# A decoder layer on one Trainium2 core: the causal mask of the scores written by ScalarE instead of by mask matmuls

## The chip, the core and the metric

The kernel runs on one core of a Trainium2 chip. A core has five engines that run their own instruction streams and meet at semaphores: TensorE (PE in the profile; its weight loads are listed as PEld), VectorE (DVE), ScalarE (ACT), GpSimd (POOL) and SyncE (SP), which here only starts transfers. The metric is the device time of one execution in microseconds, the median of several runs.

## The reference

A batch of 64 sequences of 128 tokens, 128 wide, goes through one decoder layer: a causal convolution, a minimal GRU and a feed-forward block (the mixer), a cross-attention, and a mixture of experts, each with a residual and a layer norm. The change is in the cross-attention: 16 heads of width 64, 128 queries against 120 context rows, with a causal mask that adds -1e10 above the diagonal before the softmax. Cut to that part:

```python
q = (query @ Wq + bq).reshape(B, T, H, Dk)          # query = x, T = 128
k = (key @ Wk + bk).reshape(B, S, H, Dk)            # key = value = context, S = 120
v = (value @ Wv + bv).reshape(B, S, H, Dv)
q = q * (1.0 / jnp.sqrt(jnp.asarray(Dk, q.dtype)))
scores = jnp.einsum('bthd,bshd->bhts', q, k)
causal = jnp.tril(jnp.ones((T, S), scores.dtype))
scores = scores + NEG_INF * (1.0 - causal)
attn = jax.nn.softmax(scores, axis=-1)
ctx = jnp.einsum('bhts,bshd->bthd', attn, v).reshape(B, T, H * Dv)
out = ctx @ Wo + bo
```

## The kernel before, in words

The 64 sequences are worked in 16 groups of four. Three stages run as a software pipeline: in one body the group `b` is in attention, the next group `a = b + 1` is in the mixer, and the group before, `c = b - 1`, is in the mixture of experts. The `pipeline` helper (L198) calls `body(a, b, c)` for each engine; 14 of the 16 bodies with a group in attention have all three stages. There is no scheduler: the order of the work on each engine is the order of the calls in that engine's `body`, written out by hand, and each engine issues strictly in that order.

The attention of a group has a projection part (24 projections, L353, evicted from PSUM by ScalarE for even numbers and by VectorE for odd ones, L650 and L916) and then ten steps `s` = 0 to 9. The eight steps 0 to 7 each make one score pair `p = s`: a sequence (p // 2) and one half of its heads. The two PSUM banks `sE` and `sO` (called `score_banks`) hold four heads each, 4 x 120 columns. What a step does, by engine, as far as the change bears on it:

- TensorE, `body` L499: the transposes of the normalized probabilities of pair s - 2 (`b_probs_T`, L396), in even steps the transposes of the experts' output (`c_act_T`, L483), then `b_scores(b, s)` (L373), in step 5 the hidden-state product of the GRU (`a_hid`, L291), then the probabilities times the values of pair s - 2 (`b_pv`, L409), in even steps the experts' down projection (`c_down`, L490), then the experts' up projections (`c_up`, L464), then mixer work (in step 1 `a_pw`, L277, in step 3 a transpose `a_norm_T`), and in odd steps the output projection (`b_wo`, L426). `b_scores` waits until ScalarE has finished the probabilities of the pair before in both banks, writes the mask into each bank with one bfloat16 matmul of an identity with the mask, 480 columns wide (L385), and adds the scores with eight fp32 matmuls (L390).
- VectorE, `body` L1084: copies the transposed probabilities to SBUF (`b_probs_T`, L947), takes the negated row maximum of both score banks (`b_max`, L941), adds a bias to the attention heads (`b_heads_T`, L961), takes reciprocals (`b_recips`, L957), does the experts' gating (`c_experts`, L1054), and mixer pieces: the convolution (`a_conv`, L848) in step 1, the low part of a normalized transpose (`a_norm_low`, L831) in step 3, the GRU's drive (`a_gru_drive`, L868) in step 5. The order within a step is such that the copies for pair s - 2 stand first in step s, behind all that VectorE has to do in step s - 1.
- ScalarE, `body` L730: the exponentials of a pair, bank by bank (`b_probs`, L675: four exponentials with a running sum per bank), the experts' tanh (`c_tanh`, L715: in odd steps between the two banks, in even steps behind the second), the eviction of the experts' transposes in even steps (`c_actT`, L723), and mixer pieces at the end of a step: `a_norm` (L600) ahead of step 0 and in step 3, `a_conv` (L617) in step 0, the squares `a_sums` in step 2, `a_gate` in step 4, `a_hid` (L630) in step 5.
- GpSimd: scales the probabilities by the reciprocals (`b_normal`, L1245) and weights the experts' activations (`c_weight`, L1256). At the start of the program it builds the identity and the mask (L1172 to L1182).

The waits around the change read as follows in the kernel before:

```python
if p:
    pe.wait_ge(sem["probs"], upto("probs", b, 2 * p - 1))
for r in range(2):
    mm(score_banks[r][:, 0:4 * S], identb[:], maskb[:].unsqueeze(1).to_broadcast([P, 4, S]),
       start=True, stop=False, skip_group_check=True)
```

Of the kernel before, what the change touches and what calls it, by code (L numbers as in the profile page):

```python
# [18 lines left out]
ACT = mybir.ActivationFunctionType  # L19
# [6 lines left out]
P = 128  # L26
# [4 lines left out]
S = 120  # L31
# [9 lines left out]
PAIRS = 2 * SEQ  # L41
# [16 lines left out]
    "gru_sum": 1, "gelu": 4, "mixer": 2,  # L58
    "ln1_stats": 4, "ln1_mv": 4, "ln1_eps": 1, "ln1_rstd": 1, "ln1_out": 4, "x1T_hi": 1, "x1T": 1, "x1_bo": 1,

    "ctx_hi": 1, "ctx_split": 1, "proj": 24, "proj_act": 12, "proj_dve": 12, "scores": 16, "negmax": 16, "probs": 16,
    "probsT": 16, "probsT_sb": 16, "rinv": 16, "normal": 16, "pv": 8, "headsT_sb": 8,
    "wo": 4, "attn_sum": 4, "ln2_stats": 4, "ln2_mv": 4, "ln2_eps": 4, "ln2_rstd": 4, "ln2_out": 4,

# [16 lines left out]
def layer_kernel(nc, x, ctxT, w_pw, w_gru, w_ff1, w_ff2, cols, rows, w_q, w_k, w_v, w_o, w_g, w_u, w_rs, w_d, w_sd, out):  # L81
    with ExitStack() as ctx:  # L82
# [3 lines left out]
        sem = {n: ctx.enter_context(nc.semaphore(n)) for n in [*PER_GROUP, *ONCE]}  # L86

        def later(g):

            return not (isinstance(g, int) and g == 0)  # L90

        def upto(name, g, k=0):

            return g * PER_GROUP[name] + (k + 1) * (16 if name.endswith(("loaded", "stored")) else 1)

        def whole(name, g):

            return g * PER_GROUP[name] + PER_GROUP[name]
# [73 lines left out]
        score_banks = [sE, sO]  # L172

        def seqs(ap, n=SEQ):
            return ap.rearrange("p (b n) -> p b n", b=n)
# [67 lines left out]
        def _(pe):  # L243
            mm = nc.tensor.matmul
            pe.wait_ge(sem["mixer_weights"], MIXER_WEIGHTS)
            pe.wait_ge(sem["ident"], 1)
            pe.wait_ge(sem["identb"], 1)
            pe.wait_ge(sem["mask"], 1)

            def turn(dst, src):  # L250
                return nc.tensor.transpose(dst, src, ident[0:src.shape[0], 0:src.shape[0]])  # L251
# [121 lines left out]
            def b_scores(b, p):  # L373
                q, half = p // 2, p % 2
                if p == 0:
                    pe.wait_ge(sem["proj_act"], upto("proj_act", b, 14 // 2))
                    pe.wait_ge(sem["proj_dve"], upto("proj_dve", b, 15 // 2))
                elif p == 1:
                    pe.wait_ge(sem["proj_act"], upto("proj_act", b, 18 // 2))
                    pe.wait_ge(sem["proj_dve"], upto("proj_dve", b, 19 // 2))  # L380
                if p:

                    pe.wait_ge(sem["probs"], upto("probs", b, 2 * p - 1))
                for r in range(2):
                    mm(score_banks[r][:, 0:4 * S], identb[:], maskb[:].unsqueeze(1).to_broadcast([P, 4, S]),  # L385
                       start=True, stop=False, skip_group_check=True)
                for i in range(4):
                    j = 4 * half + i
                    for r in range(2):
                        ins = mm(score_banks[r][:, i * S:(i + 1) * S], qT[r * DK:(r + 1) * DK, j, q * T:(q + 1) * T],  # L390
                                 kT[r * DK:(r + 1) * DK, j, q * S:(q + 1) * S], start=False, stop=True,
                                 skip_group_check=True)
                        if i == 3:
                            ins.then_inc(sem["scores"], 1)
# [172 lines left out]
        def _(act):  # L567
            f = nc.scalar.activation
            act.wait_ge(sem["gammas"], 1)
            act.wait_ge(sem["bq8"], 1)  # L570

            def w_high(names):
                for n in names:
                    if n in LATE_LOADS:
                        act.wait_ge(sem[f"{n}_in"], 16)
                    f(split[n][0][:], raw[n], ACT.Copy).then_inc(sem["w_hi"], 1)
# [73 lines left out]
            def b_project(b, lo, hi):  # L650
                for n in range(lo, hi):
                    if n % 2:
                        continue
                    act.wait_ge(sem["proj"], upto("proj", b, n))
                    src = proj_banks[n]
                    kind, j = projections[n]
                    if n == 12 and not later(b):
                        act.wait_ge(sem["w_lo"], len(SPLIT))
                    if n == 0:

                        if later(b):
                            act.wait_ge(sem["scores"], whole("scores", b - 1))
                    if n == 8:

                        if later(b):
                            act.wait_ge(sem["pv"], whole("pv", b - 1))
                    if kind == "v":
                        ins = f(vv[:, j // 2, (j % 2) * 512:(j % 2) * 512 + 512], src[0:S, :], ACT.Copy)
                    elif kind == "k":
                        ins = f(kT[:, j, :], src[:, 0:SW], ACT.Identity, bias=c_(f"bk{j}"))  # L670
                    else:
                        ins = f(qT[:, j, :], src[:], ACT.Identity, bias=c_(f"bq{j}"), scale=DK ** -0.5)
                    ins.then_inc(sem["proj_act"], 1)

            def b_probs(b, p, r):  # L675
                if p >= RING:

                    act.wait_ge(sem["probsT"], upto("probsT", b, 2 * (p - RING) + 1))
                else:
                    if later(b):  # L680
                        former = max(m for m in range(PAIRS) if m % RING == p)
                        act.wait_ge(sem["probsT"], upto("probsT", b - 1, 2 * former + 1))
                act.wait_ge(sem["negmax"], upto("negmax", b, 2 * p + r))
                for i in range(4):
                    ins = f(pr[:, p % RING, r, i, :], score_banks[r][:, i * S:(i + 1) * S], ACT.Exp,  # L685
                            bias=nm[:, p % 2, r, i:i + 1], accum_out=rsum[:, p % 2, r, i, :])
                ins.then_inc(sem["probs"], 1)
# [42 lines left out]
            def body(a, b, c):  # L730
                A, B, C = a is not None, b is not None, c is not None

                if B:
                    b_project(b, 4, 6)
                if C:
                    c_x2T(c)
                if A:
                    a_sums(a, 0)
                if B:
                    b_project(b, 6, 8)  # L740
                if B:
                    b_project(b, 8, 9)
                    a_x1T(b)
                if C:
                    c_shared(c)
                if B:
                    b_project(b, 9, 13)
                if C:
                    c_router(c)
                if B:  # L750
                    b_project(b, 13, 18)
                    b_probs(b, 0, 0)
                    b_project(b, 18, 20)
                if C:
                    c_sharedT(c)
                if B:
                    b_probs(b, 0, 1)
                if A:
                    a_norm(a, 0)
                for s in range(PAIRS + LAG):  # L760
                    even = s > 1 and s % 2 == 0
                    if C and even:
                        c_actT(c, s // 2 - 1)
                    if B and 0 < s < PAIRS:
                        b_probs(b, s, 0)
                    if C and s < PAIRS and s % 2:
                        c_tanh(c, s)
                    if B and s == 1:
                        b_project(b, 22, 23)
                    if B and 0 < s < PAIRS:  # L770
                        b_probs(b, s, 1)
                    if B and s == 0:
                        b_project(b, 20, 21)
                    if C and s < PAIRS and s % 2 == 0:
                        c_tanh(c, s)
                    if A:
                        if s == 0:
                            a_conv(a)
                        elif s == 2:
                            a_sums(a, 1)  # L780
                            if not later(a):
                                w_high(SPLIT[2:5])
                        elif s == 3:
                            a_norm(a, 1)
                        elif s == 4:
                            a_gate(a)
                        elif s == 5:
                            a_hid(a)
                        elif s == 7:
                            a_sums(a, 2)  # L790
                            if not later(a):
                                w_high(SPLIT[5:])
                        elif s == 8:
                            b_project(a, 0, 2)
                            a_norm(a, 2)
                            b_project(a, 2, 4)
                        elif s == 9:
                            for k in range(FCH):
                                a_gelu(a, k)

            pipeline(act, body)


# [544 lines left out]
```

## Time and profile before

| what | value |
|---|---|
| runs | 1743.06, 1748.45, 1751.35 us; median 1748.45 |
| span of the profiled execution | 1742.6 us (the lowest run is 1743.06) |
| PE busy | 1535.3 us, 88% of the span |
| DVE busy | 1172.2 us, 67% |
| ACT busy | 865.7 us, 50% |
| POOL busy | 724.7 us, 42% |
| mean granted TensorE clock | 0.967 of full speed |

The span runs from the first to the last instruction of one execution. A busy share is an average over the whole span. In a timeline, a line gives the start, the duration, the engine, the source line, the operation with its output and inputs, the count, and in brackets how long the engine had been idle before it and what released it. Line numbers are those of the kernel before.

### The profile page before, as it was taken

Reading aid. Unit: us, or ns where it says so; the run is one execution under the profiler, and the core shown is the slowest. Engines: PE = TensorE matmul, PEld = TensorE weight load, DVE = VectorE, ACT = ScalarE, POOL = GpSimd, SP = SyncE. Lnnn points to the kernel's source line nnn. Section 1 sums busy time; section 2 is a strip of 40 time slices with the busy share of each in tenths; the row PEclk is TensorE's granted clock in tenths of the full one; section 3 lists DMA queues with packets and bytes.
Section 4 is the critical chain, followed back from the end, with each engine's and each line's share of the span. In section 5 each row is a group of like instructions: output and inputs, shape, how many; then the busy total and the mean of one; then the engine's idle time right before and its main releaser. Section 6 shows DMA issues by size and latency. Waiting matters only on the chain. (4 is left out here: it accounts for less than half of the span.)

```text
span 1742.6 us, 35886 instructions
## 1 busy us (share of the span) xinstructions
PE 1535.3 (88%) x11552; PEld 1256.2 (72%) x11552; DVE 1172.2 (67%) x2822; ACT 865.7 (50%) x3177; POOL 724.7 (42%) x882
## 2 busy tenths in 40 slices
PE   2879998999899998998999899999989999899966
PEld 2667777777777776777777777777777777777754
DVE  2566867577685767757677685767767577686642
ACT  3645555364554545455464554545455464554421
POOL 5433534434353534525444353534534444352412
PEclk9999999999999999999999999999999999999987
DMA  3000000000000000000000000000000000000000
GB/s 132 7 7 1 6 14 5 16 2 16 1 5 14 3 15 2 3 14 3 15 2 16 1 5 14 3 15 2 3 14 3 15 2 16 1 5 3 4 4 7
DMA packets 22167, 18.08 MB, mean 10 GB/s; under 512 B 1904, under 2 KB 20912, under 8 KB 22064
## 3 DMA queue, kind: packets, MB, share of 16 engines
q1 hardware_dynamic: 22064, 17.05, 3.1%
q14 instruction: 80, 0.66, 0.1%
q8 instruction: 23, 0.38, 0.1%
HBM read 12.85 MB, written 4.19 MB: 10 GB/s over the span
## 5 line engine op out<-in xcount | busy, mean ns | idle before, releaser
L1247 POOL TENSOR_TENSOR pr<-pr,ri 128x480 f32<-128x480 f32 x256 | 254.5, 997 | 521.5 <-DVE ri L959 521.5
L685 ACT ACTIVATE pr<-sE,nm 128x120 f32<-128x120 f32 x512 | 178.0, 360 | 308.0 <-DVE nm L944 308.0
L422 PE MATMUL pvb<-pT,vv 120*64 120x128 f32 x2048 | 142.2, 282 | 75.4 <-DVE pT L955 75.3
L422 PEld LDWEIGHTS pvb<-pT,vv 120*64 120x64 f32 x2048 | 111.0, 138 | 106.3 <-issue 52.0
L685 ACT ACTIVATE pr<-sO,nm 128x120 f32<-128x120 f32 x512 | 178.7, 378 | 0.0
L1266 POOL TENSOR_TENSOR ew<-e,gw 128x512 f32<-128x512 f32 x128 | 135.7, 1060 | 87.5 <-DVE e L1066 73.6
L955 DVE COPY pT<-t 120x512 f32<-120x512 f32 x256 | 164.1, 682 | 1.3 <-PE t L251 0.9
L390 PEld LDWEIGHTS sE<-kT,qT 64*128 64x128 f32 x1024 | 123.4, 187 | 50.9 <-issue 50.9
L390 PE MATMUL sE<-kT,qT 64*128 64x120 f32 x1024 | 147.0, 284 | 0.0
L390 PE MATMUL sO<-kT,qT 64*128 64x120 f32 x1024 | 147.0, 284 | 0.0
L496 PE MATMUL m<-wd,eT_s 128*128 128x128 f32 x1024 | 136.4, 288 | 2.9 <-ACT eT_s L728 2.9
L496 PEld LDWEIGHTS m<-wd,eT_s 128*128 128x128 f32 x1024 | 124.0, 198 | 14.5 <-issue 10.3
L251 PE MATMUL t<-ident_f,pr 128*120 128x128 f32 x1024 | 133.7, 274 | 0.0
L431 PEld LDWEIGHTS pvb<-wo,hT 128*128 128x128 f32 x1024 | 124.9, 196 | 12.0 <-DVE hT L969 9.0
L431 PE MATMUL pvb<-wo,hT 128*128 128x128 f32 x1024 | 130.0, 281 | 3.1 <-DVE hT L969 3.1
L1058 DVE SCALAR_TENSOR_TENSOR et<-et,m 128x512 f32<-128x512 f32 x128 | 87.6, 685 | 57.5 <-ACT et L721 57.5
L728 ACT ACTIVATE eT_s<-m 128x512 f32<-128x512 f32 x128 | 69.7, 595 | 108.5 <-PE m L251 108.5
L390 PEld LDWEIGHTS sO<-kT,qT 64*128 64x128 f32 x1024 | 123.4, 187 | 0.0
L1252 POOL TENSOR_TENSOR ve<-mv,eps 128x1 f32<-128x1 f32 x128 | 24.4, 190 | 236.5 <-DVE mv L981 181.7
L251 PEld LDWEIGHTS t<-ident_f,pr 128*120 128x120 f32 x1024 | 117.7, 138 | 6.7 <-issue 0.2
L944 DVE TENSOR_REDUCE nm<-sE 128x4 f32<-128x480 f32 x128 | 83.4, 651 | 54.3 <-PE sO L390 54.3
L685 ACT ACTIVATION_READ_ACCUMULATOR pr<-sO,nm 128x1 f32 x512 | 115.5, 226 | 0.0
(271 smaller groups left out, 3914.5 us busy)
## 6 DMA issues: line engine op xcount, KB each, us to landing
xt<-in_x SPq DMA_DIRECT2D x16, 256.0 KB, 2.8
out_y<-y SPq DMA_DIRECT2D x64, 64.0 KB, 1.6
cT<-in_ctxT SPq DMA_DIRECT2D x16, 240.0 KB, 2.9
hT<-in_w_k SPq DMA_DIRECT2D x1, 512.0 KB, 6.6
qT<-in_w_v SPq DMA_DIRECT2D x1, 512.0 KB, 7.4
qT<-in_w_q SPq DMA_DIRECT2D x1, 512.0 KB, 8.2
wo<-in_w_o SPq DMA_DIRECT2D x1, 512.0 KB, 9.1
qT<-in_w_g SPq DMA_DIRECT2D x1, 512.0 KB, 8.8
```

The lines of the kernel that those rows point to most:

```text
L251: return nc.tensor.transpose(dst, src, ident[0:src.shape[0], 0:src.shape[0]])
L390: ins = mm(score_banks[r][:, i * S:(i + 1) * S], qT[r * DK:(r + 1) * DK, j, q * T:(q + 1) * T], kT[r * DK:(r + 1) * DK, j, q * S:(q + 1) * ...
L422: ins = mm(pvb[r * DK:(r + 1) * DK, (k // 2) * T:(k // 2 + 1) * T], vv[:, q, h * DK:(h + 1) * DK], pT[:, 4 * r + k // 2, :], start=True, s ...
L431: ins = mm(pvb[:, 0:P], hT[:, j, :], wo[:, j, :], start=(j == 0), stop=(j == NCH - 1))
L496: mm(m1[:, 0:P], eT[:, j, :], wd[:, j, :], start=(j == 0), stop=False)
L685: ins = f(pr[:, p % RING, r, i, :], score_banks[r][:, i * S:(i + 1) * S], ACT.Exp, bias=nm[:, p % 2, r, i:i + 1], accum_out=rsum[:, p % 2, ...
L728: f(eT[:, 4 * k:4 * k + 4, :], seqs(src[:]), ACT.Copy).then_inc(sem["eT_sb"], 1)
L944: V.tensor_reduce(nm[:, p % 2, r, :], seqs(score_banks[r][:, 0:4 * S]), AX_X, ALU.max, negate=True).then_inc(sem["negmax"], 1)
L955: V.tensor_copy(pT[:, 4 * k:4 * k + 4, :], seqs((t0, t1)[k][0:S, :])).then_inc(sem["probsT_sb"], 1)
L1058: V.scalar_tensor_tensor(et[:], et[:], 1.0, m0[:], ALU.add, ALU.mult).then_inc(sem["e_gate"], 1)
L1247: GP.tensor_tensor(pr[:, p % RING, r, :, :], pr[:, p % RING, r, :, :], ri[:, p % 2, r, :, :].to_broadcast([P, 4, S]), ALU.mult).then_inc(s ...
L1266: GP.tensor_tensor(seqs(ew[:, half * 512:(half + 1) * 512], 8), seqs(e3[:, n % 2, :], 8), gw[:, n // 2, 8 * half:8 * half + 8].unsqueeze(2 ...
```

## The change

ScalarE gets a new function, `b_mask(b, p, r)`: it copies the mask, repeated four times, from SBUF into the 480 columns of score bank `r`, and counts a new semaphore, `masked`. For the pairs after the first it waits for ScalarE's own exponentials of the pair before to be complete in that bank; for the first pair it waits for the eviction of the projection that had the bank (number 12 for `sE`, 13 for `sO`). `b_scores` loses the two mask matmuls and the wait on `probs`, waits for both masks instead, and its score matmuls, unchanged, have `start=False` and so add onto what the bank holds. In ScalarE's order the masks of the first pair stand between the projections 14 and 16, those of pair 1 behind the second bank's exponentials of pair 0, ahead of `a_norm`, and those of pair s + 1 behind the second bank's exponentials of pair s, for s = 1 to 6. The waits on the identity and the mask at the program's start move from TensorE to ScalarE (the mask alone).

```diff
@@ PER_GROUP @@
-    "ctx_hi": 1, "ctx_split": 1, "proj": 24, "proj_act": 12, "proj_dve": 12, "scores": 16, "negmax": 16, "probs": 16,
+    "ctx_hi": 1, "ctx_split": 1, "proj": 24, "proj_act": 12, "proj_dve": 12, "masked": 16, "scores": 16, "negmax": 16, "probs": 16,
@@ tensor @@
-            pe.wait_ge(sem["identb"], 1)
-            pe.wait_ge(sem["mask"], 1)
@@ b_scores @@
-                if p:
-
-                    pe.wait_ge(sem["probs"], upto("probs", b, 2 * p - 1))
-                for r in range(2):
-                    mm(score_banks[r][:, 0:4 * S], identb[:], maskb[:].unsqueeze(1).to_broadcast([P, 4, S]),
-                       start=True, stop=False, skip_group_check=True)
+
+                pe.wait_ge(sem["masked"], upto("masked", b, 2 * p + 1))
@@ scalar @@
+            act.wait_ge(sem["mask"], 1)
...
+            def b_mask(b, p, r):
+                if p:
+                    act.wait_ge(sem["probs"], upto("probs", b, 2 * (p - 1) + r))
+                elif r:
+                    act.wait_ge(sem["proj_dve"], upto("proj_dve", b, 13 // 2))
+                else:
+                    act.wait_ge(sem["proj_act"], upto("proj_act", b, 12 // 2))
+                f(seqs(score_banks[r][:, 0:4 * S]), maskb[:].unsqueeze(1).to_broadcast([P, 4, S]),
+                  ACT.Copy).then_inc(sem["masked"], 1)
@@ scalar body @@
-                    b_project(b, 13, 18)
+                    b_project(b, 13, 15)
+                    b_mask(b, 0, 0)
+                    b_mask(b, 0, 1)
+                    b_project(b, 15, 18)
                     b_probs(b, 0, 0)
                     b_project(b, 18, 20)
                 if C:
                     c_sharedT(c)
                 if B:
                     b_probs(b, 0, 1)
+                    b_mask(b, 1, 0)
+                    b_mask(b, 1, 1)
                 if A:
                     a_norm(a, 0)
                 for s in range(PAIRS + LAG):
...
                     if B and 0 < s < PAIRS:
                         b_probs(b, s, 1)
+                        if s < PAIRS - 1:
+                            b_mask(b, s + 1, 0)
+                            b_mask(b, s + 1, 1)
```

## Rows read from the trace of the kernel before

**Rows 1.** The page, first section: busy time of each engine.

```profile
PE 1535.3 (88%) x11552; PEld 1256.2 (72%) x11552; DVE 1172.2 (67%) x2822; ACT 865.7 (50%) x3177; POOL 724.7 (42%) x882
```

**Rows 2.** Line L422 (probabilities times values): its waits, us and times, of 128.

```profile
  DVE pT L955: 125.7, 117
```

**Rows 3.** Windows from exponential table load to gelu table load: PE, PEld, DVE, ACT, POOL, clock.

```profile
560.59:639.76 79.17, 72.49 (x589) 59.42 (x588) 60.49 (x141) 42.22 (x173) 36.62 (x45) 0.98 0.01 4
...
874.92:952.57 77.65, 70.98 (x589) 58.33 (x588) 60.52 (x141) 42.23 (x173) 36.62 (x45) 1.00 0.01 4
```

**Rows 4.** Timeline of PE, step 4 of the group at 874.92: masks and first score.

```profile
907.86 0.37 PE L385 MATMUL sE<-mask_b,ident_b 128*128 128x480 bf16 x1
908.07 0.37 PE L385 MATMUL sO<-mask_b,ident_b 128*128 128x480 bf16 x1
908.36 0.37 PE L390 MATMUL sE<-kT,qT 64*128 64x120 f32 x1
```

**Rows 5.** Groups by line, shape and duration: ScalarE instructions, minimum/median/maximum ns.

```profile
L721 ACT ACTIVATE et<-m x128: 597/600/618, 156.5 to 1728.0; 128x512 f32<-128x512 f32 x128
...
L576 ACT ACTIVATE wv_s_hi<-qT x1: 1045/1045/1045, 22.7 to 22.7; 128x1024 fp32r<-128x1024 f32 x1
...
L621 ACT ACTIVATE cv<-xc,col x16: 814/843/878, 15.3 to 1507.4; 128x512 f32<-128x512 f32 x16
```

**Rows 6.** Timeline of ACT, step 4: two evictions in a row.

```profile
907.69 1.09 ACT L728 ACTIVATE eT_s<-m 128x512 f32<-128x512 f32 x2 [1.74 <-PE m L251]
```

**Rows 7.** Timeline of ACT, DVE and PE, steps 0 to 2.

```profile
880.86 0.70 ACT L615 ACTIVATE xc<-ma,col 128x512 f32<-128x512 f32 x1
...
882.55 0.69 DVE L1058 SCALAR_TENSOR_TENSOR et<-et,m 128x512 f32<-128x512 f32 x1 [0.50 <-ACT et L721]
...
886.68 1.16 PE L282 MATMUL ma<-pw,cv 128*128 128x128 f32 x8 [0.63 <-DVE cv L853]
...
889.78 1.09 PE L251 MATMUL m<-ident_f,ew 128*128 128x128 f32 x8 [1.07 <-POOL ew L1266]
```

**Rows 8.** Timeline of ACT and PE, steps 2, 3 and 6: tanh and probabilities times values.

```profile
896.72 0.60 ACT L721 ACTIVATE et<-m 128x512 f32<-128x512 f32 x1 [0.78 <-PE m L257]
...
901.37 1.09 PE L422 MATMUL pvb<-pT,vv 120*64 120x128 f32 x16 [1.62 <-DVE pT L955]
...
933.08 0.60 ACT L721 ACTIVATE et<-m 128x512 f32<-128x512 f32 x1 [1.03 <-PE m L257]
```

**Rows 9.** Timeline of ACT, DVE and PE, steps 3 and 4.

```profile
905.24 0.71 ACT L615 ACTIVATE nT_hi<-ma,col 128x512 fp32r<-128x512 f32 x1
...
906.08 0.75 DVE L838 SCALAR_TENSOR_TENSOR nT_lo<-ma,col,nT_hi 128x512 fp32r<-128x512 f32 x1 [0.50 <-ACT nT_hi L615]
...
907.59 1.29 DVE L955 COPY pT<-t 120x512 f32<-120x512 f32 x2
...
909.45 1.09 PE L422 MATMUL pvb<-pT,vv 120*64 120x128 f32 x16
```

**Rows 10.** Timeline of ACT, DVE and PE, steps 5 and 6.

```profile
923.33 0.62 ACT L634 ACTIVATE hin<-ma 128x512 f32<-128x512 f32 x1
...
923.98 0.96 DVE L870 TENSOR_SCALAR hin<-hin 128x512 f32<-128x512 f32 x1 [0.31 <-ACT hin L634]
...
927.31 1.29 DVE L955 COPY pT<-t 120x512 f32<-120x512 f32 x2
...
928.65 1.09 PE L422 MATMUL pvb<-pT,vv 120*64 120x128 f32 x16 [1.35 <-DVE pT L955]
```

**Rows 11.** Waits of PE: us in total, times, longest us.

```profile
PE ma L251 <- DVE x L912: 34.3, 12, 3.2
```

**Rows 12.** Timeline of PE between two groups: the wait for the mixer's norm.

```profile
968.64 1.10 PE L251 MATMUL ma<-ident_f,x 128*128 128x128 f32 x4 [2.86 <-DVE x L912]
```

**Rows 13.** Windows of 4 us, columns as in rows 3: granted clock after two waits.

```profile
588.00:592.00 4.00, 4.00 (x21) 3.07 (x18) 2.02 (x5) 2.86 (x16) 0.99 (x2) 0.62 0.00 0
...
972.00:976.00 4.00, 4.00 (x10) 3.06 (x10) 1.85 (x6) 0.94 (x3) 3.44 (x3) 0.50 0.00 0
```

## The prediction

> **What bounds the kernel now.** I read the busy line of the page first. PE is busy 88% of the span, ACT 50% [rows 1]: that invites the reading that any matmul taken from PE shortens the run. The second view speaks against it. The waits of the line that multiplies probabilities by values (pv from here on) show that PE stood before it, for VectorE's copies of the transposed probabilities, in 117 of its 128 times, 125.7 us in all [rows 2]. The third view, windows from one group's exponential table load to its gelu load, gives 77.65 us for the attention steps of a group, with PE busy 70.98 [rows 3]. Of the 13 such stretches of full groups twelve lie within 0.03 us of this one; the thirteenth is 79.17, and there the granted clock is 0.98 instead of 1.00. A stretch that repeats so closely is a chain that crosses engines, so I followed it in the timelines of one group, step by step.
>
> In the odd steps it goes so: ScalarE's work at the end of a step, VectorE's work on that, then VectorE's copies for the next step, which stand behind it in VectorE's order, then pv on PE. In step 3, `a_norm` on ScalarE starts at 905.24 with no idle time before it, VectorE's next instruction had waited 0.50 us for it, the copies follow at 907.59 and pv at 909.45 [rows 9]. In step 5 the same with the GRU's tanh: 923.33, then 923.98 after 0.31 idle, copies at 927.31, pv at 928.65 after PE had idled 1.35 [rows 10]. ScalarE's 50% is thus no reserve in these places.
>
> **The change part by part.** *Removed from PE:* two mask matmuls per pair. The first starts 0.21 us before the second, and the second 0.29 before the first score [rows 4]. The 0.29 holds the step to the half-height score tiles, which some full-height matmul will still precede; so I take 2 x 0.21 = 0.42 us per pair, between 0.42 and the whole 0.50. It counts only where PE is not waiting afterwards.
>
> *Added to ScalarE:* two copies of 480 columns per pair. No row shows ScalarE writing PSUM. The nearest are its PSUM reads of 512 columns, 600 ns alone and 1.09 us for two in a row [rows 5, 6]; a second 512 columns cost 1045 - 600 = 445 ns, 0.87 ns per column [rows 5]. Two in a row with 480 columns: 1.09 - 2 x 32 x 0.87/1000 = 1.03 us until the second is complete; they overlap with their neighbours, so ScalarE's queue moves back by about M = 0.95 us. Lower bound: the columns alone, 2 x 0.42 = 0.83. Upper: the dearest 512-column row, 843 ns, twice: 1.69. An added instruction gives no gain, so nothing lies below 0.83. I take 0.95, as the PSUM rows are nearest. The masks need not wait for the exponentials: the second bank's are complete while the first mask runs. The Trainium skill, page "ScalarE: Activation LUTs", section "Step-by-step: what each stage is for", says that ScalarE writes PSUM faster than SBUF; every ScalarE row here writes SBUF, so no run shows it. By it M would lie below 0.95, and the last rival below says what that does.
>
> *The wait of the scores:* PE now waits for both masks. They are ready about 1.05 us after the exponentials. For pair 4 those end at 905.24, so the masks at 906.3, and PE comes at 907.86 [rows 9, 4]. I expect PE to stop there only in pair 1, whose masks come behind two evictions and all of pair 0's exponentials, at about 880.86 - 0.42 + 1.05 = 881.5 [rows 7]; the next links hide that stop.
>
> *What is queued behind the masks on ScalarE, step by step* (L is how late PE is against before):
>
> - Projections: the masks of pair 0 delay one eviction behind which the table load waits; the scores of pair 0 come 0.42 earlier. Cover: the table load ends 0.7 us before the first exponential.
> - Steps 0 to 1: the masks of pair 1 stand before `a_norm`, one eviction, the tanh and `a_conv`, with ScalarE busy throughout from 880.86 [rows 7]. VectorE's gating had waited 0.50 for that tanh and then runs without a gap through the convolution that PE waited 0.63 for and the experts' activations that it waited 1.07 for [rows 7]. So L = M - 0.42 = 0.53.
> - Step 2: PE is spared 0.42, L = 0.11. The masks stand before the tanh, which had waited 0.78 for PE [rows 8]; 0.95 - 0.78 = 0.17 comes through. L = 0.28. pv of step 3, which waited 1.62 for the copies [rows 8], is that late too: the 0.42 of step 3 only lengthens the wait.
> - Steps 3 to 4: the masks stand before `a_norm`, which was not waiting for PE: 0.28 + 0.95 = 1.23 late. VectorE follows it, and with it the copies. Before, they ended at 907.59 + 1.29 = 908.88, 0.57 before pv; 0.05 of that is signalling [rows 9, 10]. L = 1.23 - 0.52 = 0.71. Here the spared 0.42 vanishes in a new wait.
> - Steps 4 to 5: the tanh has the same 0.78 of idle and PE is late itself; L stays 0.71.
> - Steps 5 to 6: the masks stand before `a_hid`; 0.71 + 0.95 = 1.66 for VectorE, the copies and pv, which already waited 1.35. L = 1.66.
> - Steps 6 to 7: the tanh had idled 1.03 [rows 8], enough for 0.95. After step 6 no masks. L = 1.66 at the end.
>
> The start of the program costs nothing: GpSimd builds the mask while the first loads still run. With 14 full bodies: 14 x 1.66 = 23 us. The first and last bodies lack a stage, and I count nothing for them. By the bounds of M: at 0.83 the same steps give some 1.2 us per group, 17 us; at 1.69 the tanh of steps 2 and 4 and of step 6 come late as well, some 5.9 per group, 82 us.
>
> *TensorE's clock.* PE's idle time before pv of step 6 grows from 1.35 to 1.35 + 0.42 + 0.95 = 2.7 us. A wait of that size stands between the groups: 2.86 us [rows 12], twelve times, up to 3.2 [rows 11], and behind that one the granted clock is 0.50 for a whole window, the lower of the two levels, 1.2 instead of 2.4 GHz [rows 13]. Within the attention steps the clock fell once, behind a pv wait of step 3 of 1.62 us: 0.62 for 4 us [rows 13], and that group took 79.17 - 77.65 = 1.52 us longer [rows 3]. So I count one such fall per group, 14 x 1.52 = 21 us. The Trainium skill, page "TensorE: Matmul & The Clock Gate", section "Part 1: The HAM clock gate (the warmup mystery)", calls the slow clock the default that activity releases; the rows agree, and by it a longer wait is likelier to end at the slow clock.
>
> **Sum.** 1742.6 + 23 + 21 = 1787 us against the profiled span. The lowest run is 1743.06 and the median 1748.45, 0.3% above the span; I forecast 1790, between the span's sum and that of the median (1793).
>
> **The rivals.**
> 1. *The clock does not fall* in the longer waits. For it: pv waits of 1.6 us went by without one in twelve of 13 stretches. Against it: 2.7 us is nearer to the 2.86 that did it. 1742.6 + 23 = 1766; with the median's offset up to 1771.
> 2. *PE is the bound after all*: 128 x 0.42 = 54 us come off, 1690. For it: 88% busy. Against it: the 117 waits for VectorE [rows 2], and the stretches' constancy. It ends on the faster side, and the place that decides is ScalarE's queue in steps 0, 3 and 5: per group the sum is 3M - 0.42 - 0.42 - 0.52 (with the masks of the other steps hidden), which turns at M = 0.45 us, 0.23 per mask. The 0.83 of the columns alone says no. If instead the order of ScalarE and VectorE had slack that these timelines hide, the gain would be that of PE.
> 3. *A cheap mask*: if writing PSUM were about twice as quick as all SBUF rows, M = 0.45, the gains and delays cancel, and the clock has no reason to fall: 1743 to 1752. This is what the skill's rule on ScalarE's writes would make at its strongest. Nothing in the rows bears out a factor of two.
>
> **Chances.** Forecast with the clock falling 0.52 and rival 1 0.29, so 0.81 slower by more than 0.5% (about what a measurement of this kernel can tell from no change, 9 us); no difference (rival 3) 0.11; faster 0.08. The range has to reach through rival 1 and to a second fall of the clock per group (1787 + 21 = 1808) and half of the way to a dearer mask: 1750 to 1820. It leaves out the faster case and part of rival 3, and a little above.
>
> **What the changed profile would show.** Right: the stretch between table loads grows to 79 to 81 us in nearly every full group; ACT busy up by about 256 x 0.57 = 146 us; PE's waits for the copies at pv well above 125.7 us; almost no wait of the scores for the masks but in pair 1; VectorE idle for `a_norm` and `a_hid` in steps 3 and 5 longer by about 0.9 each; clock below 1.00 within the stretches. Wrong: a stretch under 77.6, masks below 0.3 us each, or pv waits unchanged. PE waiting for masks in most steps would mean a price far above 0.95.

## The result, and the profile after

The changed kernel takes 1820.2 us (median of 4 runs, 1815.62 to 1820.81) against 1749.19 for the kernel before, run on the same chip: 1.0413 times as long, with a 95% interval of 1.0382 to 1.0443. The profiled execution has a span of 1813.7 us and a mean granted clock of 0.934, against 1742.6 and 0.967. The forecast of 1790 had the sign right; the time lies 0.2 us above the range. One execution each of e3 (1922.55 us), of e4 (3516.42) and of the kernel before beside them (1810.39) was slow: the ratios below leave these three out, the medians do not.

The busy line of the page, beside [rows 1]:

```profile
PE 1534.3 (85%) x11296; PEld 1279.8 (71%) x11296; DVE 1168.4 (64%) x2822; ACT 985.8 (54%) x3433; POOL 722.5 (40%) x882
```

PE issues 256 matmuls less and is busy for as long as before (1535.3). What it was spared has come back as longer matmuls, a first sign of the clock. ScalarE has 256 instructions and 120 us more.

The new line on ScalarE, grouped by line and shape (minimum, median and maximum ns), with two lines that say who waited for it (us, times); then the waits of the line that multiplies probabilities by values, L416 now, beside [rows 2]:

```profile
L677 ACT ACTIVATE sE<-mask_b x128: 564/610/634, 61.2 to 1717.8; 128x480 f32<-128x480 bf16 x128
L677 ACT ACTIVATE sO<-mask_b x128: 564/608/632, 61.7 to 1718.3; 128x480 f32<-128x480 bf16 x128
...
  PEld sE L384: 21.4, 30
  PE sE L384: 12.5, 20
...
  DVE pT L968: 207.0, 146
```

A mask takes 0.61 us, PE seldom waits for one (12.5 us in 20 waits), but the waits for VectorE's copies have grown from 125.7 to 207.0 us. Both of these totals add up the waits of two queues, the matmuls' (PE) and the weight loads' (PEld), so 117 and 146 are not counts out of 128. The matmuls alone, before and after (us in total, times, longest us):

```profile
PE pvb L422 <- DVE pT L955: 75.3, 77, 2.5
PE pvb L416 <- DVE pT L968: 122.9, 92, 2.7
```

Windows from exponential table load to gelu table load, beside [rows 3]; the first is a group with one disturbance, the second is like eight others within 0.1 us:

```profile
580.39:660.44 80.05, 69.18 (x573) 57.95 (x572) 60.10 (x141) 48.82 (x187) 36.53 (x45) 0.98 0.01 3
...
1123.99:1206.15 82.16, 70.75 (x573) 59.59 (x572) 60.09 (x141) 48.82 (x187) 36.52 (x45) 0.96 0.01 3
```

77.65 us have become 82.16, and the clock, which was 1.00 in twelve of the 13 stretches, is 0.96 in twelve of them.

Timelines of ACT, DVE and PE in that group, steps 3 to 6, beside [rows 8 to 10]:

```profile
1150.48 1.97 PE L416 MATMUL pvb<-pT,vv 120*64 120x128 f32 x16 [2.08 <-DVE pT L968]
...
1155.80 0.59 ACT L677 ACTIVATE sE<-mask_b 128x480 f32<-128x480 bf16 x1
1156.29 0.59 ACT L677 ACTIVATE sO<-mask_b 128x480 f32<-128x480 bf16 x1
1156.79 0.71 ACT L610 ACTIVATE nT_hi<-ma,col 128x512 fp32r<-128x512 f32 x1
...
1157.62 0.75 DVE L851 SCALAR_TENSOR_TENSOR nT_lo<-ma,col,nT_hi 128x512 fp32r<-128x512 f32 x1 [1.48 <-ACT nT_hi L610]
...
1159.14 1.29 DVE L968 COPY pT<-t 120x512 f32<-120x512 f32 x2
...
1160.48 1.09 PE L416 MATMUL pvb<-pT,vv 120*64 120x128 f32 x16 [0.80 <-DVE pT L968]
...
1175.35 0.62 ACT L629 ACTIVATE hin<-ma 128x512 f32<-128x512 f32 x1
...
1176.00 0.92 DVE L883 TENSOR_SCALAR hin<-hin 128x512 f32<-128x512 f32 x1 [1.29 <-ACT hin L629]
...
1180.63 1.67 PE L416 MATMUL pvb<-pT,vv 120*64 120x128 f32 x16 [2.71 <-DVE pT L968]
1182.23 3.07 PE L490 MATMUL m<-wd,eT_s 128*128 128x128 f32 x16
```

Read downward: the two masks stand 0.49 us apart, so a pair moves ScalarE's queue by 0.98 us, and VectorE's waits behind `a_norm` and `a_hid` grow by 0.98 each (0.50 to 1.48, 0.31 to 1.29). In step 3 pv now starts after 2.08 us of idle, not 1.62, and itself takes 1.97 us instead of 1.09; in step 6 the idle is 2.71, not 1.35, pv takes 1.67, and the down projection behind it 3.07 us, where it took 2.05 before:

```profile
929.67 2.05 PE L496 MATMUL m<-wd,eT_s 128*128 128x128 f32 x16
```

The same instructions take longer behind both waits, and windows of 4 us show why (columns as in rows 3, with PE alone: us, busy, granted clock):

```profile
1147.99:1151.99 4.00, 1.92 (x22) 0.78 0.06 16
1151.99:1155.99 4.00, 4.00 (x26) 0.79 0.00 0
1175.99:1179.99 4.00, 1.93 (x24) 1.00 0.00 0
1179.99:1183.99 4.00, 3.36 (x24) 0.62 0.00 0
```

There are two falls of the clock in this group, and in twelve of the 13 full groups: behind the wait of step 3 and behind that of step 6. The group at 580.39 has only the first, and only in part.

**Where the 71 us went.** The starts of pv, counted from the first score of pair 0 (875.22 before, 1123.72 after), are late by 0.61 us in step 3 (1150.48 against 901.37), 2.53 in step 4 (1160.48 against 909.45) and 3.48 in step 6 (1180.63 against 928.65); pv of step 7 is 5.08 late. The jump from 0.61 to 2.53 holds the first fall, the one from 3.48 to 5.08 the second. Over the span: the 13 stretches of full groups sum to 1010.81 us before and 1064.66 after, +53.85; the stretch of the second group of the run, ahead of them, +5.72; the twelve gaps between groups 319.38 to 325.61, +6.23; the part behind the last exponential table load +6.1; all else -0.8. That is 71.1, the difference of the spans. What part of it is queue and what part clock the trace of after alone does not say; the experiments do.

### The profile page after: what moved, and what is told of

It is laid out like the page before. It is cut to its first block and busy times, and to the rows that moved or that the text cites. A ratio compares the mean times of both kernels' runs of the same rounds, so it can differ in the third digit from the quotient of the medians.

```text
span 1813.7 us, 35643 instructions
## 1 busy us (share of the span) xinstructions
PE 1534.3 (85%) x11296; PEld 1279.8 (71%) x11296; DVE 1168.4 (64%) x2822; ACT 985.8 (54%) x3433; POOL 722.5 (40%) x882
## 5 line engine op out<-in xcount | busy, mean ns | idle before, releaser
L416 PE MATMUL pvb<-pT,vv 120*64 120x128 f32 x2048 | 156.5, 300 | 122.9 <-DVE pT L968 122.9
L416 PEld LDWEIGHTS pvb<-pT,vv 120*64 120x64 f32 x2048 | 122.0, 148 | 154.8 <-DVE pT L968 84.1
L384 PE MATMUL sE<-kT,qT 64*128 64x120 f32 x1024 | 147.5, 285 | 12.5 <-ACT sO L677 12.5
L490 PE MATMUL m<-wd,eT_s 128*128 128x128 f32 x1024 | 153.1, 311 | 2.7 <-ACT eT_s L733 2.7
L490 PEld LDWEIGHTS m<-wd,eT_s 128*128 128x128 f32 x1024 | 140.1, 219 | 16.2 <-issue 11.9
L982 DVE TENSOR_TENSOR hT<-pvb,col 128x512 f32<-128x512 f32 x128 | 87.7, 685 | 46.7 <-PE pvb L416 44.5
L726 ACT ACTIVATE et<-m 128x512 f32<-128x512 f32 x128 | 77.6, 606 | 70.6 <-PE m L255 67.3
```

Of the source, the lines that this page charges most:

```text
L416: ins = mm(pvb[r * DK:(r + 1) * DK, (k // 2) * T:(k // 2 + 1) * T], vv[:, q, h * DK:(h + 1) * DK], pT[:, 4 * r + k // 2, :], start=True, s ...
L490: mm(m1[:, 0:P], eT[:, j, :], wd[:, j, :], start=(j == 0), stop=False)
L726: f(et[:], m0[:], ACT.Tanh, scale=0.5).then_inc(sem["e_tanh"], 1)
L982: V.tensor_tensor(hT[:, 4 * half:4 * half + 4, :], seqs(pvb[:]), c_(f"bv{4 * half}", 4).unsqueeze(2).to_broadcast([P, 4, T]), ALU.add).the ...
```

## The experiments

My theory had two terms, ScalarE's queue and the clock. The rivals were that the queue alone makes the delay (the clock then being a mark of it and no cause), and that PE's matmuls were the bound and something else took their gain. Four kernels ran together beside the kernel before (1749.12 us), then four more (1749.73 us).

**e1: the changed kernel with useless matmuls in two waits.** Ahead of pv of pairs 1 and 4, seven 480-column matmuls write the bank that pv will overwrite, while PE waits for the copies.

```diff
+                warm(pvb, {1: 7, 4: 7}.get(p, 0))
+                pe.wait_ge(sem["probsT_sb"], upto("probsT_sb", b, 2 * p + 1))
```

> The changed kernel with seven useless bfloat16 matmuls (the old mask product, 480 columns, into the bank that the following product overwrites) on TensorE ahead of the probabilities-times-values product of pairs 1 and 4, while TensorE waits for VectorE's copies there (2.08 and 2.71 us in the changed trace). Clock theory: the granted clock falls behind these two waits in every full group and costs 1.5 and 1.6 us each; filled, it does not fall, the stretch between the table loads goes from 82.2 to about 79.1 us, and the run from 1820 to about 1777 us (1798 if only one of the two falls goes). Rival, TensorE's work is what bounds: 14 x 0.2 us x 16 groups more, about 1865 us. Rival, the falls cost nothing because the queue of ScalarE sets the pace: 1820 us.

Measured: 1769.15 us, 1.0116 of before (1.0098 to 1.0134); clock 0.965. A stretch, and the step-3 place in it (timeline of PE):

```profile
1093.71:1172.92 79.21, 70.81 (x587) 58.24 (x586) 60.15 (x141) 48.81 (x187) 36.52 (x45) 1.00 0.01 4
```

```profile
1118.05 1.59 PE L408 MATMUL pvb<-mask_b,ident_b 128*128 128x480 bf16 x7
...
1120.11 1.09 PE L425 MATMUL pvb<-pT,vv 120*64 120x128 f32 x16 [0.47 <-DVE pT L977]
```

The same wait, filled with work whose result nobody reads: the clock stays at 1.00 in every full stretch, pv is back to 1.09 us, and 51 us of the 71 are gone. The clock is a cause, and the larger one. The queue keeps 79.21 - 77.65 = 1.56 us per group.

**e2: the kernel before without mask matmuls, and nothing in their place.** The scores stay unmasked. It shows what PE would gain if the masks cost nobody anything.

```diff
-                for r in range(2):
-                    mm(score_banks[r][:, 0:4 * S], identb[:], maskb[:].unsqueeze(1).to_broadcast([P, 4, S]),
-                       start=True, stop=False, skip_group_check=True)
...
-                                 kT[r * DK:(r + 1) * DK, j, q * S:(q + 1) * S], start=False, stop=True,
+                                 kT[r * DK:(r + 1) * DK, j, q * S:(q + 1) * S], start=True, stop=True,
```

> The kernel before with the mask left out altogether (no mask matmuls, nothing on ScalarE; the scores are not masked): what the removal from TensorE is worth when nothing is paid for it. Chain theory: the waits for VectorE's copies take most of it, about 1.26 us per group come off by the steps (pairs 0 and 2 and the down products), 18 us, 1731 us; with the clock theory the wait before the product of pair 1 grows from 1.62 to about 2.04 us, the clock falls there in every group, 14 x 1.5 = 21 us, and the run is about where it was, 1745 to 1755 us. Rival, TensorE is the bound: 128 x 0.42 = 54 us less, 1695 us.

Measured: 1761.99 us, 1.0081 of before (1.0063 to 1.0099). Less work on PE, none added elsewhere, and the kernel is slower. The profiled execution was the fastest of five (1753.35; the others 1761.84 to 1763.36), so the usual one may lose more than its trace shows. Three of its stretches, columns as in rows 3:

```profile
241.36:317.80 76.44, 67.72 (x573) 57.11 (x574) 60.45 (x141) 42.22 (x174) 36.70 (x45) 1.00 0.02 5
...
767.82:845.77 77.95, 69.25 (x573) 58.22 (x574) 60.54 (x141) 42.33 (x173) 36.66 (x45) 0.98 0.01 4
...
873.03:952.64 79.61, 70.92 (x573) 59.84 (x574) 60.53 (x141) 42.35 (x173) 36.67 (x45) 0.96 0.01 4
```

With the clock held a group would gain 77.65 - 76.44 = 1.21 us from all 16 mask matmuls (their time on PE is 8 x 0.42 = 3.4 us: two thirds vanish in the waits of [rows 2]). It is held in one stretch of 13; each fall takes 1.5 to 1.7 us back. This is the whole ceiling of the change in a full group, and it does not cover one fall.

**e3: the changed kernel with the mask matmuls kept as well.** ScalarE's copies and waits stay; the first matmul of a bank overwrites what ScalarE wrote.

```diff
                 pe.wait_ge(sem["masked"], upto("masked", b, 2 * p + 1))
+                for r in range(2):
+                    mm(score_banks[r][:, 0:4 * S], identb[:], maskb[:].unsqueeze(1).to_broadcast([P, 4, S]),
+                       start=True, stop=False, skip_group_check=True)
```

> ScalarE writes the masks as in the changed kernel and TensorE waits for them, but TensorE then writes the mask again with its own matmuls as before: the price of ScalarE's part without the gain on TensorE. Queue theory: 0.98 (steps 0 to 1) + 0.20 (step 2) + 0.46 (step 3) + 0.98 (step 5) = 2.6 us per full group, 37 us, 1786 us; the wait of pair 4 grows to about 2.3 us, and if the clock falls there, 21 us more, 1807 us, that of pair 1 to about 1.8 us. Rival, ScalarE's masks are hidden and the loss comes from what TensorE no longer does: 1749 us.

Measured: 1815.23 us, 1.0383 of before (1.0361 to 1.0406). Two stretches, without and with a fall, and pv of step 6 with the down projection in each (timeline of PE):

```profile
1013.30:1093.22 79.92, 71.03 (x589) 58.29 (x588) 60.21 (x141) 48.91 (x187) 36.59 (x45) 1.00 0.01 3
...
1119.93:1201.44 81.51, 72.60 (x589) 59.86 (x588) 60.21 (x141) 48.91 (x187) 36.59 (x45) 0.98 0.01 3
```

```profile
1069.32 1.09 PE L421 MATMUL pvb<-pT,vv 120*64 120x128 f32 x16 [2.30 <-DVE pT L973]
1070.34 2.05 PE L495 MATMUL m<-wd,eT_s 128*128 128x128 f32 x16
...
1175.95 1.13 PE L421 MATMUL pvb<-pT,vv 120*64 120x128 f32 x16 [2.30 <-DVE pT L973]
1177.01 3.60 PE L495 MATMUL m<-wd,eT_s 128*128 128x128 f32 x16
```

Queue without the saving: +2.3 us per group with the clock at 1.00. The wait of step 3 is 1.67 here, nearly the 1.62 of before, and in twelve of 13 groups no fall follows it; that of step 6 is 2.30, and in nine of 13 groups one does. (The group at 253.61 fell behind step 3 instead: granted clock 0.70 from 281 to 285 us, and 1.00 from 304 to 328, around step 6.) The price of a fall is the difference of two rows with equal waits: 3.60 - 2.05 = 1.55 us. The run came out 8 us above the expectation with a fall; about half of that may be the first group of the run, which grew from 62.63 to 66.96 us at a clock of 0.90 and which I had not counted.

**e4: the changed kernel with the masks of steps 3 and 5 behind `a_norm` and `a_hid`.** Only the order on ScalarE is changed.

```diff
-                        if s < PAIRS - 1:
+                        if s < PAIRS - 1 and s not in (3, 5):
                             b_mask(b, s + 1, 0)
...
+                    if B and s in (3, 5):
+                        b_mask(b, s + 1, 0)
+                        b_mask(b, s + 1, 1)
```

> The changed kernel with the masks of steps 3 and 5 moved behind ScalarE's mixer pieces of these steps (the normalization and the tanh of the GRU). Queue theory: 0.86 and 0.96 us per full group come back, 25 us, 1795 us; the wait of pair 4 falls from 2.7 to about 1.8 us and the clock falls there no longer, 14 x 1.6 = 22 us more, 1772 us. Rival, the masks are late for TensorE as they are: it then waits for them in steps 4 and 6 and the run stays at 1820 us or above.

Measured: 1773.02 us, 1.0126 of before (1.01 to 1.0152). A stretch, and pv of steps 3 and 6:

```profile
1098.26:1177.12 78.86, 69.11 (x573) 58.15 (x572) 60.12 (x141) 48.78 (x188) 36.69 (x45) 0.98 0.01 4
```

```profile
1124.75 1.98 PE L416 MATMUL pvb<-pT,vv 120*64 120x128 f32 x16 [2.08 <-DVE pT L971]
...
1153.20 1.09 PE L416 MATMUL pvb<-pT,vv 120*64 120x128 f32 x16 [1.75 <-DVE pT L971]
```

Four instructions per group in another place, and 47 us are gone: the queue delay of steps 3 and 5, and with it the long wait and the fall of step 6 (2.71 to 1.75, pv at 1.09). The wait of step 3, 2.08, is untouched, and so is its fall, in all 13 groups. This is the clearest evidence that there are two falls, each behind a wait of its own.

**e5: the kernel before with useless matmuls between the groups.** Eleven of them stand ahead of the transposes that wait for the mixer's norm [rows 11, 12].

```diff
             def a_x1_T(a):
+                pe.wait_ge(sem["mixer"], upto("mixer", a, 1))
+                warm(ma, 11)
```

> The kernel before, with eleven useless bfloat16 matmuls (the mask product, 480 columns, into the bank that the following transposes overwrite) on TensorE in the wait for the mixer's norm between two groups, which is 2.8 us long and followed by the low clock in 12 groups. Clock theory: the stretch from gelu load to exponential load goes from a mean of 26.6 us in these groups to about 24.2 (what the one such stretch with a granted clock of 1.00 took in the run with filled waits), 12 x 2.4 = 29 us, 1720 us. Rival, the norm and not the clock sets that stretch: 1749 us, or 2 us per group more.

Measured: 1726.82 us, 0.9885 of before (0.9861 to 0.9909). The gaps take 24.0 to 24.5 us at a clock of 1.00, where before they took 26.6 in the mean. The expectation of 1720 missed what the fill costs where no fall stood: the first stretch of a full group starts 4.2 us later than before (251.56 against 247.39). Two of the 13 stretches lost the clock (79.20 and 79.22 us); the other eleven are as before, 77.63 to 77.68.

**e6: e2 with useless matmuls ahead of pv of pairs 1, 3 and 4.**

```diff
+                warm(pvb, {1: 7, 3: 4, 4: 5}.get(p, 0))
```

> The kernel without any mask, as before, with useless matmuls in the waits for the copies of pairs 1 (seven), 3 (four) and 4 (five). Clock theory: the stretches go from 77.9 and 79.6 us to 76.4, what the one undisturbed stretch without the mask took, about 2.3 us x 13 = 30 us, 1731 us, which is the 1.2 us per group that the chain theory gives for the removal. Rival: 1762 us as without the filling, or above for the added matmuls.

Measured: 1716.67 us, 0.9825 of before (0.9802 to 0.9848). All 13 stretches lie between 76.36 and 76.40 us at a clock of 1.00. Sixteen matmuls per group added to e2 take 45 us off it. The sixteen mask matmuls had thus done a second service in the kernel before, beside writing the mask: without them the waits ahead of pv are longer (2.02 for 1.62 in step 3), and the clock falls. The time is 14 us lower than expected. The stretches gave what was forecast (1021.72 to 992.98 us in sum, 28.7 for 30); what was not forecast is that the twelve gaps between groups shrank too, from 324.41 to 311.15 us, most of them at a granted clock of 0.93 instead of 0.87.

**e7: a version with the mask on ScalarE that beats both kernels.** From e4, pair 1 goes back to mask matmuls (ScalarE has no slack there), and the fills of e6 and e5 are added.

```diff
+                if p == 1:
+                    pe.wait_ge(sem["probs"], upto("probs", b, 1))
+                    for r in range(2):
+                        mm(score_banks[r][:, 0:4 * S], identb[:], maskb[:].unsqueeze(1).to_broadcast([P, 4, S]),
+                           start=True, stop=False, skip_group_check=True)
+                else:
+                    pe.wait_ge(sem["masked"], upto("masked", b, 2 * p - 1 if p else 1))
```

> ScalarE's masks where they are covered, by the queue theory: pairs 0, 2, 3, 5 and 7 as in the changed kernel, pairs 4 and 6 behind the mixer pieces, pair 1 with the old mask matmuls on TensorE; and useless matmuls in the waits for the copies of pairs 1, 3 and 4 and in the wait between two groups. Queue and clock theory together: the stretch with late masks took 78.85 with one fall of the clock (1.5), less 0.98 for pair 1: 76.4; with 24.2 between the groups 100.6 a group against 104.2 before, 47 us less in all, 1702 us. Without the queue theory (masks cost where they are): no better than the kernel before with the filled gap, 1720 us.

Measured: 1709.75 us, 0.9778 of before (0.9758 to 0.9798). A gap and the stretch behind it:

```profile
1133.67:1157.88 24.21, 23.67 (x150) 18.62 (x150) 12.71 (x37) 12.18 (x27) 7.76 (x9) 1.00 0.08 22
1157.88:1234.21 76.33, 71.44 (x591) 58.44 (x590) 60.28 (x141) 47.79 (x185) 36.72 (x45) 1.00 0.01 4
```

The stretch equals that of e6, where the mask costs nothing at all: where ScalarE has idle time, the mask is free. It is 17 us better than e5, which keeps all mask matmuls and has the gap filled. e5 was not tried with the pv waits filled too, but eleven of its 13 stretches have the clock at 1.00 as they are and still take 77.65 us, so that filling could give back little more than its two falls, about 3 us. The 8 us above the expectation lie outside the groups it was worked out from: the first full stretch starts 4.7 us later than before (252.06 against 247.39), and the part behind the last exponential table load is 4.5 us longer.

**e8: the changed kernel, its order untouched, with the fills of e1 and e5.**

> The changed kernel with its masks where they stand, useless matmuls in the waits of pairs 1 and 4 and in the wait between the groups. Clock theory: 1769 us of the run with the two waits filled, less 12 x 2.4 = 29 us, 1740 us; the rest of the distance to the kernel before with its gap filled (1720 us) is the queue of ScalarE alone, about 1.6 us per full group, 22 us. Rival, the falls of the clock between the groups are paid elsewhere: 1769 us.

Measured: 1752.82 us, 1.0019 of before (1.0005 to 1.0032). Every full stretch is 79.22 to 79.26 us at a clock of 1.00. Nearly half of the miss of 13 us is what the fills cost early, where the clock did not fall: the first full stretch starts 5.6 us later than in e1 (255.18 against 249.58). Held against e5, which has nearly the same gaps, e8 prices ScalarE's queue: 1752.82 - 1726.82 = 26 us, e5's two falls and the fills of two more waits included, and per full group, with the clock at 1.00 in both, 79.23 - 77.65 = 1.58 us.

## Why the prediction was right in sign and short in size

With e8 the 71 us split as follows. *Queue*: 13 x 1.58 = 20.5 us in the full stretches and 2.3 in the second group (76.08 in e8 against 73.82), 22.8 in all. *Clock in the stretches*: 53.85 - 20.5 = 33.3 and 79.54 - 76.08 = 3.5, together 36.8. *Gaps*: 6.2, of which e5 and e8, with nearly equal gaps once the clock is held (24.17 and 24.32 us in the mean), show that it is the clock's too. *Behind the last exponential table load*: 6.1. Of this 4.5 stand behind the start of the last pv, where no mask is written any more; the same 204 matmul rows run there at a lower mean clock (windows of before and after, columns as in rows 3):

```profile
1669.90:1742.62 72.72, 45.90 (x204) 35.93 (x204) 21.55 (x66) 11.35 (x21) 12.04 (x18) 0.76 0.01 4
...
1736.48:1813.65 77.17, 50.49 (x204) 39.85 (x204) 21.54 (x66) 11.56 (x21) 12.03 (x18) 0.68 0.01 4
```

That puts most of this part with the clock too, but no run fills the waits there, so it is not shown by experiment.

- **The price of a mask** (0.95 us per pair forecast) was 0.98. The rows it was taken from read PSUM and write SBUF, a mask does the reverse; that the two came out alike is in part luck. ScalarE's busy time rose by 120 us, not 146: two masks in a row start 0.49 us apart and each takes 0.59, so they overlap more than I had allowed. The Trainium skill, page "ScalarE: Activation LUTs", section "Step-by-step: what each stage is for", says that ScalarE writes PSUM faster than SBUF. No run here shows that: 480 columns into PSUM took 610 ns, 512 columns into SBUF 600 [rows 5], and as the two also read from different places, they do not decide it.
- **The queue, step by step**, held to 0.04 us but in step 3. e8, with the clock held, shows it by itself. From its first score of pair 0 (1083.68) pv stands here:

```profile
1110.36 1.09 PE L427 MATMUL pvb<-pT,vv 120*64 120x128 f32 x16 [0.47 <-DVE pT L979]
...
1119.00 1.09 PE L427 MATMUL pvb<-pT,vv 120*64 120x128 f32 x16 [0.89 <-DVE pT L979]
...
1139.16 1.09 PE L427 MATMUL pvb<-pT,vv 120*64 120x128 f32 x16 [0.28 <-DVE pT L979]
```

  Against before that is 0.53 us late in step 3, 1.09 in step 4 and 2.05 in step 6. The forecast's L is against a score of pair 0 that comes 0.42 earlier, so 0.42 is taken off: 0.11 in step 3 (forecast 0.28), 0.67 in step 4 (0.71), 1.63 in step 6 (1.66). The term of 23 us measured 22.8.
- **PE's wait for masks** showed where it was said to: 16 of the 20 waits stand in pair 1, 0.4 us each in the full groups.
- **A reading that was wrong**: that PE stood before pv "in 117 of its 128 times, 125.7 us in all" counts the matmuls' and the weight loads' waits together. The matmuls waited 77 times, 75.3 us. The argument against PE as the bound needs only that many. And at M = 1.69 the forecast's own terms add up to about 6.2 us per group, not 5.9; only the upper end of the range drew on that.
- **The step that failed** is in "Step 2" and in the clock's part. The text had pv of step 3 waiting 1.62, said that "the 0.42 of step 3 only lengthens the wait", and then counted one fall per group, at step 6. The lengthened wait, 2.08, lost the clock as well, in every full group of e4 and after (in one of them in part); the row that should have warned was its own [rows 3, 13]: at 1.62 that very wait had already lost the clock once in 13 groups. I had this second fall only as the range's upper end. The clock term of 21 us measured 36.8 in the stretches, and 6.2 more in the gaps, which the sum had put at nothing.
- **Rival 1** (no fall, 1766 to 1771) is what e1 made of the kernel: 1769. Its mechanism is real, but the waits as they stand do lose the clock.
- **Rival 2** (PE is the bound, 1690) is excluded by e2 and e6: with the matmuls gone for nothing the time rose, and with the clock held too a full group gained 1.27 us (77.65 to 76.38) of the 3.4 that they take on PE. **Rival 3** (a mask at 0.45) falls with the 0.98.

The range ended at 1820 since it took a second fall together with a dearer mask; the mask was not dearer, but the gaps and the end of the span took 12 us that no case had.

## What to carry to other kernels

When matmuls are taken from an engine that waits for others, write down every wait of it that will grow, and price each by the slowest outcome that the trace shows behind a wait of about that size; a wait that lost the clock once may lose it every time when it is longer (1.62 us: one group of 13; 2.08 us: all 13). Work moved to an engine at 50% lands in its queue, so what matters is who waits for the next instruction behind it: e4 moved four instructions a few places and gave back two thirds of the loss. And where matmuls wait for another engine, a few useless ones in the wait are worth a trial (e1, e5, e6: 51, 23 and 45 us).

## What the runs showed of the hardware that I had not expected

Taking work off TensorE, with nothing added elsewhere, made the kernel 0.8% slower (e2), and each kernel with useless matmuls added was faster than the same kernel without them. The length of a wait does not decide alone whether the clock falls: 1.62 us lost it once in 13 groups before, 2.30 in nine of 13 in e3, 2.02 in step 3 of e2 in twelve, and 1.76 in step 6 of e2 in six of 13, where the 1.75 of e4 in the same step lost it in none. The group at 580.39 of the changed kernel kept the clock behind a wait of 2.71 us, though step 3 had cost it part of a fall (pv at 1.37 us). What else decides was not settled. The Trainium skill, page "TensorE: Matmul & The Clock Gate", section "HAM oscillation — how this bites in real kernels", describes a wait that recurs in each turn of a loop and pays for the slow clock each time; step 3 of the changed kernel and of e4 agrees, and a whole fall costs about 1.5 us there.

The gaps between the groups of e1 show the price in three sizes, for the same work (windows, columns as in rows 3):

```profile
859.67:883.85 24.18, 21.47 (x139) 17.63 (x139) 12.72 (x37) 12.18 (x27) 7.76 (x9) 1.00 0.07 22
...
963.06:988.77 25.71, 23.03 (x139) 18.92 (x139) 12.78 (x37) 12.18 (x27) 7.75 (x9) 0.93 0.07 21
...
1172.92:1199.99 27.07, 24.08 (x139) 20.03 (x139) 12.89 (x37) 12.21 (x28) 7.71 (x9) 0.87 0.06 20
```

The mean granted clock of the gap and its length go together, 1.00 with 24.18 us and 0.87 with 27.07; the instructions are the same 139 matmul rows.
